# A mixture-of-experts step loop: 79 steps instead of 80, a longer straight head and tail, and the low-half weight work of VectorE spread over 14 steps

## What is computed

```python
h = _layernorm(x, axis=-1) * (1 + cb) + sb
_, idx = lax.top_k(biased, K)                    # K = 4 of E = 16 experts
def step(y, ew):
    wg, wu, wd, c = ew
    h = jax.nn.silu(xf @ wg.T) * (xf @ wu.T)
    return (y + h @ wd.T * c[:, None], None)
y, _ = lax.scan(step, y0, (Wg, Wu, Wd, coeff.T))
z = jax.nn.silu(xf @ Sg.T) * (xf @ Su.T) @ Sd.T
x = x + gb * (y + z).reshape(shape)
```

## Time and profile before

| | |
|---|---|
| runs | 627.23, 631.28, 631.92 us; median 631.28 |
| profiled execution, span | 630.8 us |
| mean granted TensorE clock | 0.894 |
| TensorE busy | 520.9 us (83%) |
| TensorE weight load busy | 490.1 us (78%) |
| VectorE busy | 402.5 us (64%) |
| ScalarE, GpSimd busy | 279.1 us (44%), 298.4 us (47%) |

### The profile page before, as it was taken

The page is one execution under the profiler, slowest core; times in us unless marked ns, Lnnn a source line. Parts: engine busy times, 40 slices in busy tenths (PEclk is TensorE's granted clock), DMA queues, the critical chain, the costliest instruction groups (busy, mean ns, idle before and its releaser), DMA issues. The chain is left out here.

```text
span 630.8 us, 13294 instructions
## 1 busy us (share of the span) xinstructions
PE 520.9 (83%) x3587; PEld 490.1 (78%) x3588; DVE 402.5 (64%) x1154; ACT 279.1 (44%) x740; POOL 298.4 (47%) x337
## 2 busy tenths in 40 slices
PE   1597991899999999999853068799999999999897
PEld 0287891799998898898842057699998999998896
DVE  3697731323568768769777199677776777774543
ACT  1252542223644544635325274355554555553232
POOL 5644520200104446445566499634443444447893
PEclk9798996557999999999955559799999999999899
DMA  7135688427776458462275653244443444446931
GB/s 221 47 110 171 209 211 244 130 70 177 193 173 182 143 143 215 129 168 75 94 234 197 234 181 94 69 125 127 125 125 110 128 134 127 124 143 249 415 146 51
DMA packets 63668, 98.41 MB, mean 156 GB/s; under 512 B 10084, under 2 KB 48867, under 8 KB 62263
## 3 DMA queue, kind: packets, MB, share of 16 engines
q1 hardware_dynamic: 50504, 58.37, 34.3%
q0 software_dynamic: 9184, 32.66, 13.8%
q10 hardware_dynamic: 3918, 6.67, 3.3%
HBM read 60.84 MB, written 40.17 MB: 160 GB/s over the span
## 5 line engine op out<-in xcount | busy, mean ns | idle before, releaser
L1572 POOL DMA_INDIRECT ys_scr<-h,ids_st x60 | 61.6, 1027 | 73.5 <-DVE h L1626 71.2
L109 PE MATMUL GU<-gu_hi,xT 128*128 x320 | 86.9, 354 | 5.2 <-DVE lo L1655 3.1
L144 POOL DMA_INDIRECT xs_scr<-h,slot_u x64 | 62.4, 975 | 55.7 <-PE TB L1194 26.7
L109 PE MATMUL YP<-dn_hi,aT 88*128 x320 | 69.1, 308 | 4.9 <-DVE aT L1611 4.8
L1618 DVE TENSOR_TENSOR h_act<-GU,g_act 128x176 f32<-128x176 f32 (+1 forms) x96 | 35.5, 370 | 57.2 <-ACT g_act L1490 56.2
L1204 PE MATMUL O<-raw,prob 128*128 128x99 f32 x512 | 71.2, 289 | 0.0
L823 ACT ACTIVATE prob<-TB 128x512 f32<-128x512 f32 x64 | 38.2, 597 | 71.5 <-PE TB L1194 70.7
L1497 ACT ACTIVATE aT<-HT 88x256 fp32r<-88x256 f32 (+1 forms) x96 | 38.1, 398 | 69.5 <-PE HT L1728 69.4
L1204 PEld LDWEIGHTS O<-raw,prob 128*128 128x128 f32 x512 | 66.7, 205 | 0.0
L109 PEld LDWEIGHTS GU<-gu_hi,xT 128*128 128x128 f32 x320 | 54.3, 198 | 6.3 <-issue 6.3
L109 PEld LDWEIGHTS YP<-dn_hi,aT 88*128 88x128 f32 x320 | 49.1, 191 | 11.2 <-issue 7.2
(11 more groups left out here) (226 smaller groups left out, 1291.2 us busy)
## 6 DMA issues: line engine op xcount, KB each, us to landing
x_st<-xs_scr SPq DMA_DIRECT2D x80, 144.0 KB
dn_hi<-k_scr SPq DMA_DIRECT2D x48, 192.0 KB, 3.8
planes<-ys_scr POOLq DMA_DIRECT2D x8, 1024.0 KB, 17.4
k_scr<-k_ev SPq DMA_DIRECT2D x8, 768.0 KB, 4.8
dn_hi<-q_scr SPq DMA_DIRECT2D x24, 256.0 KB, 4.4
q_scr<-q_ev SPq DMA_DIRECT2D x8, 512.0 KB, 3.0
raw<-in_egu SPq DMA_DIRECT2D x8, 352.0 KB
raw<-in_x SPq DMA_DIRECT2D x36, 64.0 KB, 2.7
```

The source lines that it names most:

```text
L109: mm = eng.matmul(out, a, b, start=(i + j == 0), stop=(i == len(pairs) - 1 and j == 2))
L144: eng.indirect_dma_start(T["xs_scr"], bass.IndirectOffsetOnAxis(ap=T["slot_u"][:, par, t % 2, k:k + 1], axis=0), T["h2"][:, row, :], None) ...
L1572: eng.indirect_dma_start(ys, bass.IndirectOffsetOnAxis(ap=ids_st[:, r:r + 1].bitcast(U32), axis=0), results(r % 8), None).then_inc(sent[q] ...
```

## The change

Three numbers of `for_steps` change, and with them where steps are written out: 18 + 2 x 24 + 13 = 79 steps. The straight head now reaches beyond step 15, so that each of the first 16 steps waits for its own expert's low half and none for all 16. VectorE makes the same eleven low halves, in steps 0, 1, 3, 4, 5, 7, 8, 9, 11, 12 and 13. Because 79 is odd, buffer numbers of the shared expert's tiles are now taken from NS + n instead of n.

```diff
-UNROLL, HEAD, TAIL = 32, 12, 4
+UNROLL, HEAD, TAIL = 24, 18, 13
...
+LOW_STEPS = (0, 1, 3, 4, 5, 7, 8, 9, 11, 12, 13)
...
-            if isinstance(s, int) and LO_AHEAD + s < NE:
-                gu_low(LO_AHEAD + s)
+            if isinstance(s, int) and s in LOW_STEPS:
+                gu_low(LO_AHEAD + LOW_STEPS.index(s))
...
-            if isinstance(s, int) and s < HEAD:
-                eng.wait_ge(gu_lo, NE if s == HEAD - 1 else s + 1)
+            if isinstance(s, int) and s < NE:
+                eng.wait_ge(gu_lo, s + 1)
...
-            if isinstance(s, int) and 2 <= s < HEAD:
-                eng.wait_ge(dn_lo, NE if s == HEAD - 1 else s - 1)
+            if isinstance(s, int) and 2 <= s < NE + 2:
+                eng.wait_ge(dn_lo, s - 1)
...
-            eng.wait_ge(sent[p], 32 + 16 * (NS // 2))
+            eng.wait_ge(sent[p], 32 + 16 * len([s for s in range(NS) if s // 2 % 2 == p]))
...
-            w, p2 = NS + n, n % 2
+            w, p2 = NS + n, (NS + n) % 2
             shared_gate_up(w, p2)
             if n < TILES - 2:
-                transpose_x(w + 2, (n + 2) % 4, (w + 2) // 4 + 1)
+                transpose_x(w + 2, (w + 2) % 4, (w + 2) // 4 + 1)
```

More of the change, by code:

```diff
@@ L1437, in load_h2 @@
                 eng.wait_ge(picked, NS + n - 3)
-            eng.dma_start(x_st[:, n % 4, 0:D], tile_of(T["h2_scr"], n)).then_inc(xs_ld[n % 4], 16)
+            t = (NS + n) % 4
+            eng.dma_start(x_st[:, t, 0:D], tile_of(T["h2_scr"], n)).then_inc(xs_ld[t], 16)
         def load_x(s, t):
@@ L1537, in _ @@
         for n in range(TILES):
-            gate(NS + n, n % 2, GU[0], SH_I)
+            p2 = (NS + n) % 2
+            gate(NS + n, p2, GU[0], SH_I)
             if n < TILES - 2:
-                x_hi(NS + n + 2, n % 2)
+                x_hi(NS + n + 2, p2)
             if n == 0:
-                a_hi(NS - 1, 1, FH, 2)
+                a_hi(NS - 1, 1 - p2, FH, 2)
             else:
-                a_hi(NS + n - 1, 1 - n % 2, P, SH_K)
-        a_hi(NS + TILES - 1, 1, P, SH_K)
+                a_hi(NS + n - 1, 1 - p2, P, SH_K)
+        a_hi(NS + TILES - 1, (NS + TILES - 1) % 2, P, SH_K)
     @block.gpsimd
@@ L1632, in keep_late @@
             eng.wait_ge(add_ld[n // 4], 16)
-            eng.tensor_tensor(to_add[:, n, :], YP[n % 2][:, 0:D], to_add[:, n, :], ALU.add).then_inc(z_late, 1)
+            eng.tensor_tensor(to_add[:, n, :], YP[(NS + n) % 2][:, 0:D], to_add[:, n, :], ALU.add).then_inc(z_late, 1)
         def add_late(n):
@@ L1638, in add_late @@
             eng.wait_ge(fold, 3 * (n - KEPT) + 3)
-            done = eng.tensor_tensor(to_add[:, n, :], YP[n % 2][:, 0:D], planes[:, n, 0, :], ALU.add)
+            done = eng.tensor_tensor(to_add[:, n, :], YP[(NS + n) % 2][:, 0:D], planes[:, n, 0, :], ALU.add)
             done.then_inc(final if n % 2 else z_late, 1)
@@ L1690, in _ @@
         for n in range(TILES):
-            p2 = n % 2
+            p2 = (NS + n) % 2
             gating(NS + n, p2, GU[1][:, 0:SH_I], SH_I)
@@ L1702, in _ @@
             if n == 0:
-                a_lo(NS - 1, 1, FH, 2)
+                a_lo(NS - 1, 1 - p2, FH, 2)
             else:
@@ L1708, in _ @@
         add_late(TILES - 2)
-        a_lo(NS + TILES - 1, 1, P, SH_K)
+        a_lo(NS + TILES - 1, p2, P, SH_K)
         add_late(TILES - 1)
@@ L1800, in _ @@
             if n == 0:
-                transpose_a(w - 1, 1, FH, 2)
+                transpose_a(w - 1, 1 - p2, FH, 2)
             else:
                 transpose_a(w - 1, 1 - p2, P, SH_K)
-        transpose_a(NS + TILES - 1, 1, P, SH_K)
+        transpose_a(NS + TILES - 1, p2, P, SH_K)
         for w in (NS + TILES - 2, NS + TILES - 1):
```

## The result

| | before | after |
|---|---|---|
| median of 20 runs each, us | 629.19 (620.83 to 631.92) | 623.66 (618.71 to 625.69) |
| profiled execution, span, us | 630.8 | 622.5 |
| step 4 begins | 379.71 | 379.23 |
| first shared tile begins | 561.68 | 553.61 |
| from there to the end of the span | 69.1 | 68.9 |

The ratio is 0.9926, 95% interval [0.9906, 0.9946]: 0.7% less, 4.7 us by the ratio and 5.5 by the medians, which is within the 1% taken above for no change. The time forecast was 622.8, the range 618.5 to 628.0, and 623.66 lies in it. Faster by over 1% had been given 0.70, the same 0.26: by the ratio it is the same.

The account below looks back on a forecast made before the run. It took TensorE to bound the loop, VectorE's low halves the early steps. 75 steps (165.4 us) plus lows, entry, wrap, exit and shared-expert subtractions put the first shared tile 8.5 earlier: span 622.3, time 622.8, range 618.5 to 628.

Parts of the forecast that it names:

- What bounds the loop: Full-speed expert steps, 413.2 to 479.4: TensorE busy 66.17 of 66.20 us, so 2.205 us a step.
- the wait for all 16: Ahead of step 11: TensorE idle 3.13 us until VectorE's last low half; 4.18 us lost, which the change removes.
- the slow clock: Behind that idle time TensorE runs at 1.2 GHz; 3.08 us lost in all, 2.75 of it in steps 11 to 13.
- The sum from step 4 on: 75 steps of 2.205 (165.4) plus 4.7, 0.55, 2.22, 0.55 and 0.1; first shared tile at 553.2, 8.5 us earlier.
- the lows: Spread low halves on VectorE: six in steps 3 to 9 cost 4.6 us, the last three 0.1; together 4.7.
- entry: Loop entry, now between full-speed steps without cover: 0.55 us taken, between 0 and 2.22.
- wrap: The loop's jump back, where ScalarE is late: kept at 2.22 us.
- exit: Leaving the loop: kept at 0.55 us.
- The low halves' two prices: VectorE's lo lasts 1.7 us beside GpSimd's subtraction in steps 3 to 9, and 0.9 in 11 to 13.
- Rival A: Gain half eaten: entry costs like the wrap (+1.7), last lows dear (+2.1); 626.6 us, chance 0.22.
- Rival B: With the shorter loop body ScalarE's code may stay, so the wrap costs 0.56; 621.1 us, chance 0.15.
- Rival C: Two-step distance makes TensorE's waits for lows of steps 11 to 13 feed back: 12.5 us, 635.3, slower; chance 0.03.

Follow-up runs that it names:

- the third pair: Third profiles of the unchanged kernel before and of the unchanged change, on one chip: spans 626.9 and 621.8 us, steps 189.78 and 184.08.
- down halves first: The changed kernel with GpSimd's subtractions for experts 8 to 15 made before its first send; ratio to the kernel before 1.0004 [0.9949, 1.006].

## Why the prediction was right and wrong

**What bounds the loop, and the wait for all 16: right.** TensorE is the bound at 2.20 us a step; the stall and the slow clock are gone when the steps wait for one expert each, and come back when the wait for all does.

**The sum from step 4 on: 0.9 too low, with errors that cancel in part.** It had 8.1 us over 75 steps of 2.205; the trace has 9.0 (174.38 - 165.4). By terms: steps 4 to 13, which hold all the low halves, cost 5.2 over plain steps, where 4.7 was taken for the lows; the four steps behind them 0.46, the waits on dn_lo, for which nothing was taken; entry 0.85 for 0.55; wrap 2.40 for 2.22; exit 0.35 for 0.55. Plain steps at 2.20 instead of 2.205 give some 0.25 back. Step 4 began 0.5 earlier than assumed, and so the first shared tile came at 553.61 for 553.2.

**The low halves' two prices: right.** lo and GpSimd's neighbours in the changed kernel:

```profile
397.44 1.28 POOL L1554 TENSOR_TENSOR lo<-raw,dn_hi 88x512 fp32r<-88x512 f32 x1
397.79 1.68 DVE L1658 TENSOR_TENSOR lo<-raw,gu_hi 128x704 fp32r<-128x704 f32 x1
...
398.88 1.44 POOL L1575 DMA_INDIRECT ys_scr<-h,ids_st  x1 [0.17 <-issue]
400.34 1.30 POOL L1554 TENSOR_TENSOR lo<-raw,dn_hi 88x512 fp32r<-88x512 f32 x1
401.80 0.98 POOL L1575 DMA_INDIRECT ys_scr<-y_st,ids_st  x1 [0.17 <-issue]
403.01 0.88 DVE L1658 TENSOR_TENSOR lo<-raw,gu_hi 128x704 fp32r<-128x704 f32 x1
...
405.31 0.88 DVE L1658 TENSOR_TENSOR lo<-raw,gu_hi 128x704 fp32r<-128x704 f32 x1
405.61 1.41 POOL L1575 DMA_INDIRECT ys_scr<-h,ids_st  x1 [0.89 <-DVE h L1629]
```

In steps 3 to 9 it lasts 1.68 to 1.87, as in the earlier trace rows, and ends 0.75 after GpSimd's subtraction (399.47 and 398.72); in 11 to 13 it lasts 0.88, as sgu_lo did. The Trainium skill (SBUF — State Buffer, Who interferes with whom), by which the loser waits for the whole instruction, agrees with these rows and with the experiment that moved GpSimd's halves. Rival A wanted the last lows dear; they were not, but it was closer than the prediction had it: GpSimd, which lags, ends its last subtraction at 401.64, only 1.4 us before the first of the last three begins.

One thing the prediction used in rival A alone, and not in the price of a low half: GpSimd hardly waits in the dear steps either. Its send (1.44), its subtraction (1.29) and some 0.2 between them make 2.9 us, the length of such a step. Whether a shorter send or subtraction would shorten these steps was not tried.

**Rival B, a cheap wrap: fell.** 2.40 us, and ScalarE's stand of 2.82 is no shorter than with the longer body. The rows it leaned on had missed two of the five packets of the second round.

**Rival C, a new stall: fell.** Two steps of distance were enough; the steps that follow the last lows take 2.3.

**The time: near by luck; the step that failed is the conversion of one profile into the median.** 622.8 was forecast and 623.66 measured, but the base was 2.1 us too high (631.28 for 629.19) and the gain 3.0 too big (8.5 for 5.5), and these nearly cancel. The prediction subtracted 8.5 from the profiled execution's own span, and the two profiled spans do differ by 8.3. But it set that span 0.5 below the median and took both for the same kind of number. In every run that has both, the time is 1.8 to 2.2 us more than the span (1.8 to 1.9 for this kernel), so that by this estimate the profiled execution of before took about 632.7: 3.5 above the median of the 20 runs and above each of them. The change's profiled execution took 624.4, 0.8 above its median. 8.3 - (3.5 - 0.8) is 5.6, what the medians show. With 5.5 of 629 the gain falls short of the 1%.

**Behind it: two terms that vary were taken as constants.** The slow clock was priced at 3.08, of which 2.75 lies in the first two steps behind the idle time. That is the dearest of those seen (2.75, 2.12 and 2.51 in three profiles of before, 1.48 with the wait put back). The other 0.33 was not the clock's for the most part: 0.2 of it is in step 23, which takes 2.41 or 2.42 in all three profiles of before, twelve steps behind the idle time and at full clock. Nor is the time between steps 4 and 10 fixed: the 4.19 lost there was 3.8 and 2.7 in the other two profiles. All the steps together take 191.94, 191.24 and 189.78 in the kernel before and 183.97, 183.95 and 184.08 in the change, so that the gain in the steps is 8.0, 7.3 and 5.7 by pairs. The prediction counted how far the runs differ as a width of its range, but not that its own trace could stand at the end of it; 0.70 for faster was too much.

**Open.** The 20 runs have no step starts, so whether the steps give 5.7 in the median run, or 7 with something given back ahead of them, as the third pair's 1.9 us there would have it, can't be told. Nor is it known why the lower level lasts 6.8 us in three executions and 3.4 in a fourth, or what decides how early in the idle time it begins.

## What to carry to other kernels

Where an engine waits once for all of something that it needs one by one, wait for each, as long as the code is straight there: one idle time of 3.1 us cost 4.2 and then 1.5 to 2.8 more by the slow clock behind it. Before a sum is turned into a time, ask where the profiled execution lies among the runs, and which of its terms are seen to vary; a gain of 1.3% read from one trace was 0.7 to 0.9% of the medians. A hardware loop of two rounds paid 3.6 us for its entry, its jump back and its exit, and writing the steps out was the biggest gain tried on top of the change.

## What the runs showed of the hardware

A wait on a semaphore that is already reached cost TensorE 0.1 us in each step, ahead of `down` (2.31 against 2.20), and nothing ahead of `gate_up`.

VectorE's and GpSimd's subtractions take turns, and either can be the one that waits. In the steps of the change GpSimd's keeps its 1.28 to 1.30 us and lo grows from 0.88 to 1.68; in "down halves first" one lo stays at 0.87 and GpSimd's subtraction beside it takes 2.13 (421.70 and 421.82 above). GpSimd's send beside a lo grows from 0.96 or 0.98 to between 1.41 and 1.47 in the change, and lo stays at 0.88 (405.31 and 405.61 above).

Of the fall of the clock behind an idle time of 3.1 us, what is paid is the part at the lower level in which TensorE works, 0.42 to 0.44 us for each microsecond of it: 2.75 us lost for 6.4 at the lower level, 1.48 for 3.4.

The stages ahead of the steps took 368 to 370 us in five profiles, and 381 to 407 in nine on other chips. DMA issues, with their KB and the median us from issue to landing, in the kernel before on the chip of the result and then on the other:

```profile
dn_hi<-k_scr SPq DMA_DIRECT2D x48, 192.0 KB, 3.8
dn_hi<-q_scr SPq DMA_DIRECT2D x24, 256.0 KB, 4.4
```

```profile
dn_hi<-k_scr SPq DMA_DIRECT2D x48, 192.0 KB, 6.8
dn_hi<-q_scr SPq DMA_DIRECT2D x24, 256.0 KB, 4.3
```

All five profiles with a first step at 368 to 370 have 3.8 to 4.0 for the first, and all nine others 6.8 or 6.9, while the second is 4.2 to 4.5 in all. In the stretch from 200 to 280 us the granted clock is 1.00 in the former and 0.77 to 0.89 in the latter. That the late loads of k let TensorE idle and its clock fall fits both rows; it was not tried.
